# Delta-rule attention with experts: the triangular inverse of a 32-token chunk split into two 16x16 substitutions and a product on TensorE

## The chip, the cores and the metric

One of the cores of one Trainium2 chip runs the whole program. The metric is the device time of one execution in microseconds; lower is better.

## What is computed

One transformer block on 4096 tokens of width 256. Its attention part is a gated delta rule with 8 heads, 8 memories ("modes") per head, keys and values of 64, in a strict recurrence over the tokens:

```python
def step(S, inp):
    q_t, k_t, v_t, b_g, b_beta = inp
    S = S * jnp.exp(b_g)[..., None, None]
    kv = jnp.einsum('mbhk,mbhkv->mbhv', k_t, S)
    dv = (v_t[None] - kv) * b_beta[..., None]
    S = S + k_t[..., :, None] * dv[..., None, :]
    o_t = jnp.einsum('mbhk,mbhkv->mbhv', q_t, S)
    return (S, o_t)
```

Keys and queries are rotated by angles that are scaled per head and mode, and normalised. Outputs of the modes are mixed, gated and projected. Then follows a layer of 8 experts with top-2 routing and a capacity of 1024 rows each. Everything is float32.

## The kernel before

The program has three blocks. The first (attention and routing) walks 32 tiles of 128 tokens; each tile is done in two **halves** `(n, hh)` of four heads, that is 8 "quads" q (a head and four of its modes; the four modes stand in four groups of 32 partitions). The program counts halves as u = 2n + hh, and v = u - 1 is the half before. A tile has four **chunks** c of 32 tokens. The second block does the experts, the third combines their rows.

Within a chunk the recurrence is solved by matrices. For each of 128 problems (4 chunks, 8 quads, 4 modes) of a half, a unit lower triangular 32x32 matrix has to be inverted, and its columns scaled by beta. `solve` (L1259) does this on VectorE with one problem per partition: L1261 transposes the 32x32 blocks of the systems from `at` into `bd`, L1263 puts beta on the diagonal in PSUM (`last_two`), and then 31 steps j each multiply a column of the system by row j of the inverse (L1270) and subtract the product from the rows below (L1272). L1275 transposes the inverse to `tt`. Two small jobs are done between steps: `clip_decays` (j = 8) and `sum_decays` (j = 16) for the next tile in halves with hh = 1, and `take_logits` (j = 12) of the tile before in halves with hh = 0; the last waits for TensorE's routing product.

In software pipelining, the half v of which `solve` has just ended goes through its four chunks while the half u is prepared. For each chunk, one chain alternates between TensorE (PE), VectorE (DVE), ScalarE (ACT) and GpSimd (POOL):

- `memory_read` (PE L572, 32 matmuls): keys times state;
- `right_sides` (DVE L1288, L1291);
- `expand_te` (ACT L797): `tt` of the chunk spread into block-diagonal `te`;
- `corrections` (PE L589 and L595, two groups g of heads): `te` times the right sides, and queries times state;
- `decayed_corrections` (DVE L1298), `take_dv` (ACT L812), `fade` (POOL L1573: decay of the state);
- `update_and_outputs` (PE L608, L616), and `update_memories` (DVE L1307, L1309), after which the state is ready for the next chunk.

Between these, each engine's program has the preparation of u woven in by hand, in the order of its function `half`: angles (`turns_mod_1`, `add_low_turns`, `turns_end`), `decays`, key rotation, `beta_decays` (L1230), `turn_keys`, `queries_for_memories` (L1248, L1249), `chunk_systems` (L1256, L1257, out of the PE products `gram`, L533). PE also copies rows over the partitions (`rows`, L508, in three pairs per half), replicates units (L517), makes `columns` (L498) of the decays that ACT has spread in `roots` (L838), and does the projections of the next tile (L482, L544, L555, L490) and the routing (L633, L638).

Each engine has a queue in order; a wait holds up all that is behind it. The products that are not the memories' own go through two rotating pairs of PSUM banks: one pair is taken by ACT (`to_act`/`take`), one by DVE (`to_dve`/`full`/`free`), each bank in turn, so that PE must wait with a product until its bank's use before last has been read. The loop body over the tiles holds `half(n, 1)` and `half(n + 1, 0)`; each engine goes back to its start after the latter.

## Time and profile before

| | before |
|---|---|
| median of 3 runs | 7000.74 us (6998.04 to 7004.32) |
| the profiled execution | 6999.14 us, its span 6997.4 us |
| busy: PE / PE weight loads | 4452.0 / 3830.1 us (64% / 55% of the span) |
| busy: DVE | 5135.8 us (73%) |
| busy: ACT / POOL | 3430.8 / 2767.8 us (49% / 40%) |
| mean granted TensorE clock | 0.817 of full speed |

Busy times are sums over one execution. Timeline rows have a start and a length in us; one row may hold several instructions. PE writes two records for each float32 matmul of the program (and two for its weights): x64 is 32 matmuls. What stands in square brackets is how long the engine was idle before the row and what released it. A granted clock of 1.00 is 2.4 GHz, of 0.50 is 1.2 GHz.

### The profile page before, as it was taken

The page shows a single profiled execution, that of the slowest core. Times are in us where ns is not written, and L with a number is a line of the kernel's source. Part 1 is how long each engine was busy: PE and PEld are TensorE (multiplying, and loading weights), DVE is VectorE, ACT ScalarE, POOL GpSimd, SP SyncE. Part 2 cuts the span into 40 slices and gives each one's busy share as a digit, 9 for nine tenths or more (in the row PEclk, how much of TensorE's full clock was granted, in tenths as well). Part 3 has the DMA queues.
Part 4 walks back from the last instruction along what each step waited for, and adds up shares of the span by engine and source line. Part 5 has one row for each costly group of instructions (what it writes and reads, how often), then busy time and mean ns, then how long its engine had stood idle before and what let it go on. Part 6 is the DMA issues. An engine that isn't in the chain of part 4 may idle for free. (4 is left out here: it accounts for less than half of the span.)

```text
span 6997.4 us, 195918 instructions
## 1 busy us (share of the span) xinstructions
PE 4452.0 (64%) x78513; PEld 3830.1 (55%) x78513; DVE 5135.8 (73%) x9800; ACT 3430.8 (49%) x6010; POOL 2767.8 (40%) x1789
## 2 busy tenths in 40 slices
PE   1666666666666666666666666666666666655993
PEld 1555555555555555555565555555555655553662
DVE  4888778888887887878888888778888888881003
ACT  1555555555555555555555555555555555542220
POOL 3444343444343443434443434434344443434003
PEclk6878878888887788888888787887878887887997
DMA  2000000000000000000000000000000000002223
GB/s 88 2 5 5 6 5 5 5 5 3 4 5 5 5 5 6 5 5 5 5 3 5 5 5 5 5 6 5 5 5 5 3 5 5 5 27 95 72 72 105
DMA packets 77479, 109.71 MB, mean 16 GB/s; under 512 B 20576, under 2 KB 66208, under 8 KB 75424
## 3 DMA queue, kind: packets, MB, share of 16 engines
q1 hardware_dynamic: 67616, 71.42, 3.2%
q0 software_dynamic: 8960, 25.39, 1.2%
q8 instruction: 672, 11.01, 0.7%
q14 instruction: 231, 1.89, 0.1%
HBM read 57.89 MB, written 38.89 MB: 14 GB/s over the span
## 5 line engine op out<-in xcount | busy, mean ns | idle before, releaser
L1573 POOL TENSOR_TENSOR state<-state,gc_end 128x512 f32<-128x512 f32 x512 | 591.5, 1172 | 1852.4 <-PE bank L595 1811.9
L589 PE MATMUL bank<-rhs,te 128*64 128x64 f32 x8192 | 412.6, 254 | 765.9 <-DVE rhs L1291 490.0
L572 PE MATMUL bank<-state,ke 128*64 128x64 f32 x16384 | 656.1, 248 | 341.0 <-DVE outT L1309 221.4
L572 PEld LDWEIGHTS bank<-state,ke 128*64 128x64 f32 x16384 | 616.8, 160 | 415.8 <-DVE state L1307 237.1
L797 ACT ACTIVATE te<-tt 32x256 f32<-32x256 f32 x1024 | 421.9, 412 | 802.6 <-DVE tt L1275 792.0
L589 PEld LDWEIGHTS bank<-rhs,te 128*64 128x64 f32 x8192 | 345.0, 163 | 844.4 <-DVE rhs L1291 795.8
L608 PE MATMUL last_two<-dvs,kte 128*64 128x64 f32 x16384 | 658.9, 241 | 180.1 <-DVE dvs L1298 180.1
L1272 DVE TENSOR_TENSOR last_two<-last_two,prod 128x31 f32<-128x31 f32 (+15 forms) x1984 | 692.4, 349 | 68.2
L847 ACT ACTIVATE ke<-kq 32x512 f32<-32x512 f32 x1024 | 642.9, 628 | 201.7 <-DVE kq L1223 188.0
L1270 DVE TENSOR_TENSOR prod<-bd,last_two 128x31 f32<-128x31 f32 (+15 forms) x1984 | 671.1, 338 | 68.3
L608 PEld LDWEIGHTS last_two<-dvs,kte 128*64 128x64 f32 x16384 | 597.2, 154 | 196.5 <-DVE dvs L1298 187.3
L533 PE MATMUL bank<-kq,ke 128*64 128x64 f32 x16384 | 536.2, 227 | 199.8 <-DVE pw L1257 111.2
L804 ACT ACTIVATE kte<-kt 32x512 f32<-32x512 f32 x1024 | 641.9, 627 | 36.5 <-PE last_two L608 17.1
L533 PEld LDWEIGHTS bank<-kq,ke 128*64 128x64 f32 x16384 | 512.6, 142 | 214.0 <-issue 125.8
L1598 POOL TENSOR_TENSOR pw<-pw,w_quad 128x1024 f32<-128x1024 f32 x64 | 122.5, 1914 | 992.3 <-DVEq L1441 992.3
L812 ACT ACTIVATE dv<-bank 128x256 f32<-128x256 f32 x512 | 188.1, 379 | 571.0 <-DVE dvs L1298 561.2
L1307 DVE TENSOR_TENSOR state<-last_two,state 128x512 f32<-128x512 f32 x512 | 354.0, 691 | 116.5 <-POOL state L1573 77.0
L508 PE MATMUL bank<-row_group,select 128*128 128x128 f32 x3072 | 417.9, 290 | 29.7 <-DVE col L1186 23.9
L508 PEld LDWEIGHTS bank<-row_group,select 128*128 128x128 f32 x3072 | 375.7, 198 | 47.7 <-DVE col L1186 24.2
L1768 DVE TENSOR_TENSOR yrow<-last_two,b_row 128x256 f32<-128x256 f32 x64 | 27.2, 424 | 503.9 <-PE last_two L1722 503.9
L1586 POOL TENSOR_TENSOR tmp<-raw,cos_t 128x1024 f32<-128x1024 f32 x64 | 151.5, 2368 | 589.7 <-ACTq L888 589.7
L595 PE MATMUL bank<-qg,state 128*64 128x32 f32 x8192 | 374.4, 240 | 0.0
(257 smaller groups left out, 10221.1 us busy)
## 6 DMA issues: line engine op xcount, KB each, us to landing
w_sb<-in_L_ffn_W_dram SPq DMA_DIRECT2D x16, 1024.0 KB, 9.5
expert_rows<-ke SPq DMA_DIRECT2D x1, 8192.0 KB, 21.9
xrows<-expert_rows SPq DMA_DIRECT2D x16, 512.0 KB, 8.4
expert_outputs<-yrow POOLq DMA_DIRECT2D x16, 512.0 KB, 3.4
xt<-_attn_hidden_states_dram SPq DMA_DIRECT2D x32, 128.0 KB, 2.9
xr<-_attn_hidden_states_dram SPq DMA_DIRECT2D x32, 128.0 KB, 2.1
x_after_attention<-xr SPq DMA_DIRECT2D x32, 128.0 KB, 1.7
xo<-x_after_attention SPq DMA_DIRECT2D x32, 128.0 KB, 3.9
```

The source lines that it names most:

```text
L508: mm = pe.matmul(b[:, ql * P:ql * P + P], select[:, b4 * 4 + ql, :], row_group[:, group, :], start=True, stop=True)
L533: mm = pe.matmul(b[s, q * 2 * C:(q + 1) * 2 * C], ke[:, c, r, q, s], kq[:, r, q, :, c * C:c * C + C], start=(r == 0), stop=(r == 1))
L572: mm = pe.matmul(bank_mem[g][s, q % 4 * DK:q % 4 * DK + DK], ke[:, c, r, q, s], state[:, hh * HQ + q, r, :], start=(r == 0), stop=(r == 1))
L589: pe.matmul(bank_mem[g][s, q % 4 * DK:q % 4 * DK + DK], te[:, q, s], rhs[:, q, :], start=True, stop=True)
L595: mm = pe.matmul(out_bank(g, side), state[:, hh * HQ + q, r, :], qg[:, r, q, c * C:c * C + C], start=(j == 0 and r == 0), stop=False)
L608: mm = pe.matmul(bank_upd[g][s, (q % 4) * P + r * DK:(q % 4) * P + r * DK + DK], kte[:, r, q, s], dvs[:, q, :], start=True, stop=True)
L797: ins = act.activation(te[s, :, 32 * m:32 * m + 32], tt[s, c, :, :], ACT.Copy)
L804: ins = act.activation(kte[s, :, :, 32 * m:32 * m + 32].rearrange("p r q f -> p (r q) f"), kt[s, :, :, c * C:c * C + C].rearrange("p r q f ...
L847: ins = act.activation(ke[s, c, :, :, 32 * m:32 * m + 32].rearrange("p r q j -> p (r q) j"), kq[s, :, :, 0, c * C:c * C + C].rearrange("p ...
L1270: ln(dve.tensor_tensor(pr, a_prob[:, j + 1:C, j:j + 1].broadcast_to([P, rows, cols]), t_prob[:, j:j + 1, 0:cols].broadcast_to([P, rows, co ...
L1272: ln(dve.tensor_tensor(below, below, pr, ALU.subtract))
L1573: pool.tensor_tensor(sv, sv, gc_end[:, vh, 4 * g:4 * g + 4, c].unsqueeze(2).broadcast_to([P, 4, 2 * DK]), ALU.mult).then_inc(sem(f"state_f ...
```

## The change

The 32x32 triangular matrix is taken as two 16x16 diagonal blocks and a lower left block. `solve` inverts both diagonal blocks side by side in 15 steps on DVE (b = 2 blocks of HC = 16), and writes them transposed (`tt_blocks`) and not (`t_blocks`). The lower left block of the inverse is the product -B inv * L * A inv. It is made for each chunk by two groups of matmuls, `cut_products` (32 matmuls, through a bank of ACT, taken by `take_cut`) and `lower_left` (32 matmuls, through a bank of DVE, taken by `finish_inverse`, which is what `tt_ready` now tells). These are put one chunk ahead of their use: chunk 0 at the end of the half of its `solve`, chunk 1 around the update of chunk 0, chunks 2 and 3 around the update of chunk 1. `queries_for_memories` goes behind `solve`, together with its PE `rows`; `sum_decays` goes behind the substitution; ACT's spread of the decays, PE's `columns` and POOL's `group_rows` go later. `take_logits` stays within `solve`, at step 8 of 15, `clip_decays` at 9. `beta_decays` is split, so that the lower 16 columns can take the mask with them. In the last block four loads of `xo` become one.

```diff
@@ tiles
-        prod = sb("prod", [P, HH * P])
+        cut = sb("cut", [P, 2, HQ, C])
...
+        at = raw[:].rearrange("p s h t -> p (s h t)").rearrange("p (c q i) -> p c q i", c=NC, q=HQ)
...
+        a_blocks = bd_flat.rearrange("p (i x j) -> p i x j", x=4, j=HC)[:, :, 0:4:3, :]
+        prod = dvs[:].rearrange("p q v -> p (q v)")
...
@@ tensor
+            def cut_products(u, c):
+                pe.wait_ge(sem("t_turned"), u + 1)
+                def emit(b):
+                    pe.sem_inc(sem("pe_held"), 1)
+                    for q in range(HQ):
+                        for s in MODES:
+                            top = slice(s.start, s.start + HC)
+                            mm = pe.matmul(b[s, q * HC:(q + 1) * HC], at[top, c, q, :], t_blocks[top, c, q, :], start=True, stop=True)
+                    return mm
+                to_act(emit)
+            def lower_left(u, c):
+                pe.wait_ge(sem("cut_ready"), 4 * u + c + 1)
+                def emit(b):
+                    pe.sem_inc(sem("pe_held"), 1)
+                    for q in range(HQ):
+                        for s in MODES:
+                            mm = pe.matmul(b[s, q * HC:(q + 1) * HC], cut[s, c % 2, q, :], tt_blocks[s, c, q, :], start=True, stop=True)
+                    return mm
+                to_dve(emit)
...
+                if not first:
+                    corrections(v, vh, 0)
                 if hh == 0:
                     columns(n)
-                if hh == 1:
-                    pe.wait_ge(sem("logits_taken"), since("logits_taken", n))
-                if not first:
-                    memory_read(v, vh, 0)
-                    corrections(v, vh, 0)
+                if not first:
+                    cut_products(v, 1)
                     update_and_outputs(v, 0)
+                    lower_left(v, 1)
                     memory_read(v, vh, 1)
                 pe.wait_ge(sem("groups_ready"), n + 1)
                 rows(hh)
                 if not first:
                     corrections(v, vh, 1)
+                    cut_products(v, 2)
+                    cut_products(v, 3)
                     update_and_outputs(v, 1)
+                    lower_left(v, 2)
+                    lower_left(v, 3)
                 replicate(u, (0, 1), to_dve)
...
-                rows(4 + hh)
...
+                rows(4 + hh)
+                cut_products(u, 0)
+                if hh == 0 and not first:
+                    pe.wait_ge(sem("logits_taken"), since("logits_taken", n))
+                memory_read(u, hh, 0)
+                lower_left(u, 0)
@@ scalar
+            def take_cut(v, c):
+                act.wait_ge(sem("t_turned"), v + 1)
+                act.activation(tt[:, c, :, 0:HC], tt_blocks[:, c], ACT.Copy, scale=upper)
+                take(lambda b: act.activation(cut[:, c % 2, :, 0:HC], b[:, 0:HQ * HC].rearrange("p (q j) -> p q j", q=HQ), ACT.Copy, scale=minus_lower))
+                act.sem_inc(sem("cut_ready"), 1)
             def expand_te(v, c):
+                act.wait_ge(sem("tt_ready"), 4 * v + c + 1)
...
@@ vector
-                for j in range(C - 1):
+                for j in range(HC - 1):
                     for do in meanwhile.get(j, ()):
                         do()
-                    rows, cols = C - 1 - j, j + 1
...
+                    rows, cols = HC - 1 - j, j + 1
+                    pr = prod[:, 0:rows * 2 * cols].rearrange("p (i b c) -> p i b c", b=2, c=cols)
+                    below = t_prob[:, j + 1:HC, :, 0:cols]
+                    ln(dve.tensor_tensor(pr, a_blocks[:, j + 1:HC, :, j:j + 1].broadcast_to([P, rows, 2, cols]),
+                                         t_prob[:, j:j + 1, :, 0:cols].broadcast_to([P, rows, 2, cols]), ALU.mult))
                     ln(dve.tensor_tensor(below, below, pr, ALU.subtract))
...
+                ln(dve.transpose(tt_blocks.rearrange("p c q i -> p i (c q)"), t_rows))
+                vec(dve.transpose(t_blocks.rearrange("p c q j -> p j (c q)"), t_prob.rearrange("p i b j -> p j b i")), "t_turned", u + 1)
+            def finish_inverse(v, c):
+                b = full()
+                free(dve.scalar_tensor_tensor(tt[:, c, :, HC:C], tt_blocks[:, c], lower,
+                                              b[:, 0:HQ * HC].rearrange("p (q i) -> p q i", q=HQ), ALU.mult, ALU.add))
+                dve.sem_inc(sem("tt_ready"), 1)
...
                 memories(right_sides, 0)
                 turns_mod_1(u)
+                memories(finish, 0)
+                add_low_turns(u)
                 memories(decayed_corrections, 0)
-                add_low_turns(u)
                 if hh == 0:
                     take_columns()
+                memories(finish, 1)
...
                 decays(u, hh, 1)
+                memories(finish, 2)
+                memories(finish, 3)
                 memories(right_sides, 2)
...
-                queries_for_memories(u, first)
...
+                solve(u, hh, first, meanwhile)
+                if hh == 1 and not last:
+                    sum_decays(n2)
+                queries_for_memories(u, first)
```

PE's order from a half's first correction to its second memory read. In the program before:

```order
L572 MATMUL bank<-state,ke 64x64 x32
L585 REGISTER_ALU
L589 MATMUL bank<-rhs,te 64x64 x8
L595 MATMUL bank<-qg,state 64x32 x8
L589 MATMUL bank<-rhs,te 64x64 x8
L595 MATMUL bank<-qg,state 64x32 x8
L608 MATMUL last_two<-dvs,kte 64x64 x16
L612 REGISTER_ALU
L616 MATMUL bank<-pw,dv 64x32 x4
L608 MATMUL last_two<-dvs,kte 64x64 x16
L616 MATMUL bank<-pw,dv 64x32 x4
L572 MATMUL bank<-state,ke 64x64 x32
```

In the changed program, from `columns` on (L671 is `cut_products`, L683 `lower_left`, L617 and L625 the update, L581 the memory read):

```order
L507 MATMUL bank<-cmat,xg 128x32 x4
L461 REGISTER_ALU
L671 MATMUL bank<-bd,raw 32x16 x32
L617 MATMUL last_two<-dvs,kte 64x64 x16
L621 REGISTER_ALU
L625 MATMUL bank<-pw,dv 64x32 x4
L617 MATMUL last_two<-dvs,kte 64x64 x16
L625 MATMUL bank<-pw,dv 64x32 x4
L683 MATMUL bank<-bd,cut 32x16 x32
L581 MATMUL bank<-state,ke 64x64 x32
```

A group of 32 small matmuls now stands before the update of chunk 0 and another behind it; `columns` has moved from ahead of the first memory read to here.

PE's order a little later, from the second correction of chunk 1 to the memory read of chunk 2. In the program before:

```order
L595 MATMUL bank<-qg,state 64x32 x8
L608 MATMUL last_two<-dvs,kte 64x64 x16
L616 MATMUL bank<-pw,dv 64x32 x4
L608 MATMUL last_two<-dvs,kte 64x64 x16
L616 MATMUL bank<-pw,dv 64x32 x4
L459 REGISTER_ALU
L517 MATMUL bank<-unit,spread 128x512 x2
L572 MATMUL bank<-state,ke 64x64 x32
```

In the changed program:

```order
L604 MATMUL bank<-qg,state 64x32 x8
L671 MATMUL bank<-bd,raw 32x16 x32
L461 REGISTER_ALU
L671 MATMUL bank<-bd,raw 32x16 x32
L617 MATMUL last_two<-dvs,kte 64x64 x16
L625 MATMUL bank<-pw,dv 64x32 x4
L617 MATMUL last_two<-dvs,kte 64x64 x16
L625 MATMUL bank<-pw,dv 64x32 x4
L468 REGISTER_ALU
L683 MATMUL bank<-bd,cut 32x16 x32
L677 REGISTER_ALU
L683 MATMUL bank<-bd,cut 32x16 x32
```

Four groups of 32 have come in between the correction of chunk 1 and `replicate` (L526 now), behind which the memory read of chunk 2 stands as before.

DVE's order from the decayed corrections of chunk 0 to the update of its memories, in the program before:

```order
L1298 TENSOR_TENSOR dvs<-bank,dec_end 128x256 x2
L1173 TENSOR_TENSOR tmp<-tmp,kq 128x1024
L1115 REGISTER_ALU
L1174 TENSOR_SCALAR tmp<-tmp 128x1024
L1115 REGISTER_ALU
L1118 REGISTER_ALU
L1186 COPY col<-bank 128x128
L1307 TENSOR_TENSOR state<-last_two,state 128x512
```

In the changed program, from the low turns on (L1353 is `finish_inverse`, L1387 the first row of `update_memories`):

```order
L1241 TENSOR_TENSOR tmp<-tmp,sin_t 128x1024
L1182 REGISTER_ALU
L1242 TENSOR_SCALAR tmp<-tmp 128x1024
L1182 REGISTER_ALU
L1377 REGISTER_ALU
L1378 TENSOR_TENSOR dvs<-bank,dec_end 128x256 x2
L1185 REGISTER_ALU
L1254 COPY col<-bank 128x128
L1191 REGISTER_ALU
L1185 REGISTER_ALU
L1353 SCALAR_TENSOR_TENSOR tt<-bd,cmat,bank 128x8x16
L1387 TENSOR_TENSOR state<-last_two,state 128x512
```

The low turns have gone ahead of the decayed corrections, and `finish_inverse` of chunk 1 has come in ahead of the update of chunk 0. `finish_inverse` of chunk 0 stands just ahead of the low turns.

## Rows read from the trace of the kernel before

**Rows 1.** The profile's page: busy us, share of the span and instructions by engine.
```profile
PE 4452.0 (64%) x78513; PEld 3830.1 (55%) x78513; DVE 5135.8 (73%) x9800; ACT 3430.8 (49%) x6010; POOL 2767.8 (40%) x1789
```
**Rows 2.** The page's costliest groups: the substitution's two operations.
```profile
L1272 DVE TENSOR_TENSOR last_two<-last_two,prod 128x31 f32<-128x31 f32 (+15 forms) x1984 | 692.4, 349 | 68.2
L1270 DVE TENSOR_TENSOR prod<-bd,last_two 128x31 f32<-128x31 f32 (+15 forms) x1984 | 671.1, 338 | 68.3
```
**Rows 3.** Timeline of DVE, queries and the substitution of an hh = 1 half.
```profile
2012.09 0.69 DVE L1248 TENSOR_TENSOR qg<-kq,bank 128x512 f32<-128x512 f32 x1 [0.20 <-PE bank L508]
...
2025.77 1.99 DVE L1261 STREAM_TRANSPOSE bd<-cos_t 128x1024 f32<-128x1024 f32 x1 [0.15 <-DVE pw L1257]
...
2028.15 0.20 DVE L1270 TENSOR_TENSOR prod<-bd,last_two 128x31 f32<-128x31 f32 x1
...
2040.43 0.42 DVE L1270 TENSOR_TENSOR prod<-bd,last_two 128x256 f32<-128x256 f32 x1
2040.88 0.43 DVE L1272 TENSOR_TENSOR last_two<-last_two,prod 128x256 f32<-128x256 f32 x1
2041.35 1.55 DVE L1144 TENSOR_TENSOR_SCAN gb<-cmat,gb 64x128 f32<-64x128 f32 x1
...
2056.22 0.43 DVE L1288 TENSOR_TENSOR bank<-bank,eg_col 128x256 f32<-128x256 f32 x1
...
2060.14 0.42 DVE L1298 TENSOR_TENSOR dvs<-bank,dec_end 128x256 f32<-128x256 f32 x1
```
**Rows 4.** Timeline of DVE, the substitution of the hh = 0 half that follows.
```profile
2119.41 1.98 DVE L1261 STREAM_TRANSPOSE bd<-cos_t 128x1024 f32<-128x1024 f32 x1
...
2136.37 0.17 DVE L1325 TENSOR_TENSOR lg<-bank,br_row 128x8 f32 x1 [6.08 <-PE bank L638]
...
2156.69 0.43 DVE L1288 TENSOR_TENSOR bank<-bank,eg_col 128x256 f32<-128x256 f32 x1 [3.33 <-issue]
```
**Rows 5.** Timeline behind both substitutions: updates and third right sides on DVE, `te` on ACT.
```profile
2065.05 0.69 DVE L1307 TENSOR_TENSOR state<-last_two,state 128x512 f32<-128x512 f32 x1
...
2079.13 0.43 DVE L1288 TENSOR_TENSOR bank<-bank,eg_col 128x256 f32<-128x256 f32 x1 [1.05 <-PE bank L572]
...
2164.53 0.69 DVE L1307 TENSOR_TENSOR state<-last_two,state 128x512 f32<-128x512 f32 x1 [0.22 <-DVE tmp L1174]
...
2056.10 1.69 ACT L797 ACTIVATE te<-tt 32x256 f32<-32x256 f32 x4 [8.97 <-DVE tt L1275]
```
**Rows 6.** Timeline of PE: small matmuls in a row, columns, memory read, first corrections.
```profile
2005.81 0.61 PE L595 MATMUL bank<-qg,state 128*64 128x32 f32 x16
2006.25 0.66 PE L589 MATMUL bank<-rhs,te 128*64 128x64 f32 x16
...
2044.46 1.91 PE L498 MATMUL bank<-cmat,xg 128*128 128x32 f32 x8 [6.96 <-ACT xg L838]
2046.30 3.68 PE L572 MATMUL bank<-state,ke 128*64 128x64 f32 x64
2057.94 1.12 PE L589 MATMUL bank<-rhs,te 128*64 128x64 f32 x16 [7.95 <-ACT te L797]
...
2061.34 1.21 PE L608 MATMUL last_two<-dvs,kte 128*64 128x64 f32 x32
```
**Rows 7.** Timeline of PE, chunk 1: update, replicate, memory read of chunk 2.
```profile
2072.06 1.13 PE L608 MATMUL last_two<-dvs,kte 128*64 128x64 f32 x32
...
2074.64 1.13 PE L517 MATMUL bank<-unit,spread 128*128 128x512 f32 x2
2076.88 1.13 PE L517 MATMUL bank<-unit,spread 128*128 128x512 f32 x2 [1.11 <-DVE dec L1195]
2077.93 2.09 PE L572 MATMUL bank<-state,ke 128*64 128x64 f32 x64
```
**Rows 8.** Busy time and granted clock by stretch, the fourth last number the clock.
```profile
2057.90:2061.00 3.10, 3.06 (x58) 3.09 (x60) 2.47 (x4) 0.33 (x1) 0.95 (x1) 0.50 0.03 5
2066.00:2080.00 14.00, 12.77 (x293) 10.81 (x293) 10.91 (x21) 9.81 (x16) 2.06 (x2) 1.00 0.01 4
```

More of the change, by code:

```diff
@@ L28 @@
 C = 32
+HC = C // 2
 NT = T // P
@@ L957, in _ @@
                 take_dv(v, c)
+                for c2 in ((1,), (2, 3), (), ())[c]:
+                    take_cut(v, c2)
                 if c < NC - 1:
```

136 lines of the change are left out of this document (79 added, 57 removed).

## The prediction

> **What bounds the kernel now.** I read the page's busy times first [rows 1]: DVE is busy 73% of the span, PE 64%, ACT 49%, POOL 40%. No engine is full, so the chain has to be followed. The page's groups name the largest thing on DVE [rows 2]: the two operations of the substitution, 671.1 + 692.4 = 1363.5 us. The timeline then says what each stretch waits for. In the substitution DVE works without a break, and the other engines are waiting for it: ACT was idle 8.97 us before it could spread `tt` [rows 5], PE 7.95 us before the corrections [rows 6]. Behind the substitution the chunk chain takes over; there DVE has its own fill work, and PE is almost full (12.77 of 14.00 us busy in one such stretch [rows 8]). So DVE sets the pace while it substitutes, and PE and DVE by turns in the chunks. Both kinds of half are needed, since they differ: with hh = 0, `take_logits` holds DVE 6.08 us within the substitution [rows 4], and the loop's turn costs another 3.33 us behind it (cause "issue").
>
> I work everything out for one pair of halves (a tile) and multiply by 31.5, as there are 63 halves with a memory half behind a substitution. The profiled execution took 6999 us, 1.6 us under the median, so no correction is due.
>
> **Part 1: what the substitution gives back.** An operation of 31 elements takes 0.20 us, one of 256 takes 0.42 or 0.43, and starts follow each other by 0.45 and 0.47 [rows 3]. That is 0.19 us (multiply) or 0.20 us (subtract) and 1.04 ns an element, start to start. The new 15 steps handle 2 x 680 = 1360 elements in each operation: 15 x 0.39 + 2 x 1360 x 1.04 ns = 8.7 us, against 23.4 for 31 steps with 5456. Two transposes of 512 elements replace one of 1024; from the 1.99 us of L1261 for 1024 elements [rows 3] I take 1.05 each.
>
> - hh = 1. Before: from the first transpose to the right sides 2056.22 - 2025.77 = 30.45 us [rows 3], and 3.15 us of queries ahead of it (four of 0.69 and their gaps [rows 3]): 33.6. After: transposes 2.4, steps 8.7, clip 1.0, transposes 2.2, scan 1.55 [rows 3], queries 3.1: 18.9. Gain 14.7.
> - hh = 0. Before: 2156.69 - 2119.41 = 37.3 [rows 4], and 3.15: 40.4. After: the routing product for `take_logits` comes out of a chain (POOL's `pw`, turns and squares, PE, ACT, PE) that starts where the substitution starts and doesn't get shorter; it lands 2136.37 - 2119.41 = 17.0 us in [rows 4]. DVE reaches step 8 after 7 us and waits 10. Then 0.2 + 4.0 (seven steps) + 2.2 + queries 3.1 + loop 3.3: 29.8. Gain 10.6.
>
> Together **-25.3 us a pair**.
>
> **Part 2: what one group of 32 small matmuls costs.** The trace has no 32x16 matmul. The nearest row is L595, which streams 32 columns: 8 matmuls took 2006.25 - 2005.81 = 0.44 us [rows 6], 55 ns each, so 32 make 1.76. Upper bound: L572, also 32 matmuls, took 2.09 us at the full clock and 3.68 at the half [rows 6, 7]. Lower bound: an estimate of half of L595's, 0.88 us, if the weights (32 columns instead of 64) are what fills those 55 ns. I take **1.75 us**, as L595 is nearest in what it streams. Rule against row: the Trainium skill (TensorE: Matmul & The Clock Gate, back-to-back issue gap) says that starts never come closer than about 25 ns however few columns; by two records a matmul that is an estimate of 1.6 us, and the sum below would be 7112 instead of 7155. The 27 ns a record of L595 agree with it.
>
> **Part 3: the first chain, from the right sides to the update of chunk 0.** Before it took 2065.05 - 2056.22 = 8.8 us (hh = 0 half) and 2164.53 - 2156.69 = 7.8 us [rows 3, 4, 5]. `tt` was whole at its start, and the low turns covered PE's update. Now the chain is: right sides and mod-1 turns 3.8 (together they fill 2056.22 to 2060.14 [rows 3]) and `finish_inverse` 0.35, since all of these stand ahead on DVE; `te` 1.7 and its signal 0.15; corrections 2061.34 - 57.94 = 3.4, at the half clock that the rows show after such a gap (0.50 [rows 8]; PE would have been idle about 5 us here); `cut_products` of chunk 1, 2.0 (between full and half clock); update, two groups, 2.5 (2072.06 to 2074.64 is 2.6 with small waits [rows 7]); `lower_left` 1.75; landing and `finish_inverse` 0.55. Sum 16.2, and with `columns` (1.9, L498 [rows 6]) 18.1. DVE has nothing to fill the wait: the low turns have gone ahead, and the update of chunk 0, though ready, is queued behind `finish_inverse` of chunk 1. Cost 9.3 + 8.4 = **+17.7 us a pair**. `finish_inverse` of chunk 0 waits for nothing: its two groups and ACT's cut lie beside the queries and right sides.
>
> **Part 4: the second chain, to the right sides of chunk 2.** Before: 2079.13 - 2065.05 = 14.1 us [rows 5]. From 2072.06 on PE ran update, replicate and memory read with one gap of 1.11 [rows 7]. Four groups come in, 7.0 us; they swallow that gap. Net 5.9, and 0.1 for the wait for a bank before the last: **+12.0 us a pair**.
>
> **Part 5: the small rest.** `beta_decays` in four pieces instead of two, 0.3 a half: **+0.6**. ACT's `take_cut`, two operations of 128 elements a chunk, lies beside PE's groups; with it gone as cover nothing else would be late, so 0. One clearing less on ACT, 0: ACT waited there. POOL's `group_rows` moves between two fades; rows of PE ask for it 3 us after the update, 0. The merged `xo` loads: SP only, and the last block waits for gathers, 0. The queue in which a wait is added is DVE's (four of `finish_inverse`), and its price is parts 3 and 4.
>
> **Sum:** -25.3 + 17.7 + 12.0 + 0.6 = +5.0 us a pair, times 31.5 = +156. **Forecast 7155 us**, 2.2% slower: DVE's saved work comes back as waits for PE. Its own range is 7020 to 7350 (group cost 1.6 to 2.05; clock after the gap).
>
> **The rivals.**
>
> *The small matmuls are cheap (faster).* Place: the six groups on the chain in each half. If a group costs 0.88 us, the first chain shrinks by 2 and the second by 2 (there DVE's decays set the end instead), 8.1 a pair: 5.0 - 8.1 = -3.1, 6900 us; with the clock staying up, 6780. It decides from 1.2 us a group, 37 ns a matmul. For it: only 32 weight columns, and L595's 55 ns double with the clock (L572: 2.09 and 3.68), as array work does and a fixed issue cost would not. Against: L589 streams twice L595's columns, and its 16 records took 0.66 us against 0.61 [rows 6], so the stream is not the bound there; whether it is the weights or a floor for each record, no row tells.
>
> *DVE stays the bound (faster by far).* If the chains of parts 3 and 4 were hidden but for the new DVE work (about 2 us a half), -25.3 + 4.6 a pair gives 6350 us. For it: the busy share. Against: DVE's order in parts 3 and 4 has nothing to cover with.
>
> *The clock stays up.* Corrections at 1.9 instead of 3.4, columns at 1.0: -3.9 a pair, leaving +1.1: 7035 us. For it: PE has shorter gaps. Against: after 7.95 us idle the clock was 0.50 [rows 8], and 5 us is nearer to that than to the 1.11 us gap at 1.00.
>
> *Row tiles hinder each other (slower by far).* The four modes of a group work in different row groups and write one bank. If each record had to end before the next starts, at about 0.2 us a record (L595's 16 records took 0.61 us, their starts spread over 0.41 of it [rows 6]), a group takes 13 us; six on the chain add 67 us a half, and the kernel ends near 11,000 us. The Trainium skill (TensorEngine Tiling (Array Packing), restrictions, PSUM pressure) says that different row tiles cannot access the same bank at once. No row here has two row tiles; every matmul before uses all 128 rows.
>
> **Numbers.** Forecast 0.52; cheap matmuls 0.22; DVE bound 0.07; clock up 0.14 (a part of it within the bounds of no change); row tiles 0.05. About 0.2% (14 us) is what a measurement of this kernel can tell from none. So faster 0.32, same 0.05, slower 0.63. The range leaves out the far cases and the tails of the near ones: 6850 to 7350.
>
> **What would show it.** Right: DVE busy falls to about 4370 us (-1363 + 490 + 110), PE's matmul records rise by 32,768 to 111,000; a DVE wait of 5 to 7 us before `finish_inverse` of chunk 1 in each half, released by PE's L683; a wait of about 3 us at the update of chunk 1 and 2.5 at the right sides of chunk 2; `take_logits` waits 10 us. Wrong: groups of 32 under 1.2 us; a clock of 1.00 in the first corrections; DVE idle less than 20 us a half.

## The result and the profile after

| | before | changed |
|---|---|---|
| median | 7002.5 us (4 runs) | 7382.9 us (4 runs, 7376.6 to 7392.9) |
| ratio | | 1.0544, 95% interval 1.0526 to 1.0563 |
| span of the profiled execution | 6997.4 us | 7374.9 us |
| mean granted clock | 0.817 | 0.794 |

The kernel got 5.4% slower; 2.2% was forecast, and the time lies above the range. The page's row that answers to [rows 1]:

```profile
PE 5202.4 (71%) x111281; PEld 4513.9 (61%) x111281; DVE 4365.2 (59%) x8200; ACT 3583.1 (49%) x6458; POOL 2749.4 (37%) x1790
```

VectorE gave back 771 us of work, and the kernel lost 377. The timeline of DVE in an hh = 1 half, from its substitution to the right sides of chunk 2 (answers to [rows 3, 5]):

```profile
2145.73 1.05 DVE L1347 STREAM_TRANSPOSE bd<-last_two 128x512 f32<-128x512 f32 x1
...
2153.48 0.43 DVE L1368 TENSOR_TENSOR bank<-bank,eg_col 128x256 f32<-128x256 f32 x1 [0.37 <-DVE qg L1319]
...
2171.50 0.35 DVE L1353 SCALAR_TENSOR_TENSOR tt<-bd,cmat,bank 128x128 f32<-128x128 f32 x1 [6.11 <-PE bank L683]
2172.08 0.69 DVE L1387 TENSOR_TENSOR state<-last_two,state 128x512 f32<-128x512 f32 x1 [0.23 <-DVE tt L1353]
...
2185.54 0.69 DVE L1387 TENSOR_TENSOR state<-last_two,state 128x512 f32<-128x512 f32 x1 [2.04 <-PE last_two L617]
...
2196.55 0.43 DVE L1368 TENSOR_TENSOR bank<-bank,eg_col 128x256 f32<-128x256 f32 x1 [4.67 <-PE bank L581]
```

I cut each half at four events of DVE: first subtraction of the substitution, first store of the right sides, update of chunk 0, first store of the right sides of chunk 2. The stretches in us, hh = 1 half / hh = 0 half (a half is named after its substitution); the upper two rows are one pair near 2000 us, the lower two the means of 61 halves (all but the first and the last two):

| | substitution to right sides | first chain | second chain | rest |
|---|---|---|---|---|
| before, one pair | 28.3 / 35.1 | 8.4 / 7.4 | 14.6 / 14.6 | 42.4 / 43.5 |
| changed, one pair | 17.5 / 28.6 | 18.1 / 16.1 | 24.9 / 23.6 | 39.9 / 38.4 |
| before, mean | 28.6 / 35.5 | 8.4 / 7.4 | 14.5 / 14.6 | 42.5 / 41.3 |
| changed, mean | 17.1 / 28.5 | 18.0 / 15.3 | 24.1 / 23.1 | 40.2 / 38.5 |

The single pair makes the chains look longer than they are on average, so the account goes by the means, and so do all lengths of chains below. The queries (3.15 us a half) moved from the rest to the first column. With them counted in both kernels, a pair gains 24.9 in the substitution, and loses 1.1 in the rest, 17.6 in the first chain and 18.2 in the second: 12.0, or 378 us in 31.5 pairs.

The second chain on PE in an hh = 1 half:

```profile
2173.14 3.68 PE L581 MATMUL bank<-state,ke 128*64 128x64 f32 x64 [1.71 <-DVE outT L1389]
2176.75 2.94 PE L517 MATMUL bank<-row_group,select 128*128 128x128 f32 x16
...
2181.61 1.21 PE L671 MATMUL bank<-bd,raw 16*32 16x16 f32 x104
2183.98 0.38 PE L671 MATMUL bank<-bd,raw 16*32 16x16 f32 x24 [1.16 <-issue]
2184.28 1.15 PE L617 MATMUL last_two<-dvs,kte 128*64 128x64 f32 x32
...
2185.47 1.96 PE L617 MATMUL last_two<-dvs,kte 128*64 128x64 f32 x32
2187.22 0.59 PE L625 MATMUL bank<-pw,dv 128*64 128x32 f32 x8
2187.74 1.05 PE L683 MATMUL bank<-bd,cut 32*32 32x16 f32 x64
2189.68 1.05 PE L683 MATMUL bank<-bd,cut 32*32 32x16 f32 x64 [0.88 <-issue]
2191.36 3.78 PE L526 MATMUL bank<-unit,spread 128*128 128x512 f32 x4 [0.63 <-DVE tt L1353]
2195.07 2.36 PE L581 MATMUL bank<-state,ke 128*64 128x64 f32 x64
```

The same stretch before:

```profile
2165.59 2.10 PE L572 MATMUL bank<-state,ke 128*64 128x64 f32 x64 [0.67 <-DVE outT L1309]
2167.62 2.05 PE L508 MATMUL bank<-row_group,select 128*128 128x128 f32 x16
...
2171.54 1.13 PE L608 MATMUL last_two<-dvs,kte 128*64 128x64 f32 x32
```

and the granted clock by stretch, changed kernel (fourth last number):

```profile
2159.60:2165.00 5.40, 5.40 (x74) 5.27 (x75) 1.10 (x3) 2.78 (x9) 2.48 (x4) 0.50 0.02 3
2165.00:2173.10 8.10, 6.43 (x209) 6.22 (x208) 1.60 (x5) 1.50 (x4) 1.27 (x5) 0.50 0.02 4
2173.10:2176.80 3.70, 3.66 (x65) 3.57 (x65) 3.23 (x6) 3.60 (x7) 0.00 (x0) 0.50 0.00 0
2176.80:2181.60 4.80, 4.80 (x81) 4.65 (x80) 1.62 (x4) 4.13 (x5) 0.66 (x1) 0.81 0.02 3
...
2187.70:2195.10 7.40, 5.88 (x137) 3.12 (x134) 3.50 (x7) 3.61 (x8) 0.00 (x0) 0.50 0.02 4
```

Before, it had been 0.50 in the first corrections and was 1.00 from the memory read of chunk 1 on:

```profile
2157.60:2161.20 3.60, 3.57 (x66) 3.52 (x66) 3.20 (x5) 0.00 (x0) 1.45 (x1) 0.50 0.00 0
2161.20:2165.60 4.40, 3.73 (x83) 3.64 (x82) 3.86 (x6) 3.25 (x8) 1.30 (x2) 0.69 0.02 4
2165.60:2169.70 4.10, 4.10 (x82) 3.86 (x82) 3.60 (x7) 3.56 (x5) 0.00 (x0) 1.00 0.01 4
```

So two things stand in the second chain. New work: the four groups take 1.21 + 0.38 + 1.05 + 1.05 = 3.7 us in this half. And old work runs at the lower clock: memory read 3.68 against 2.10, rows 2.94 against 2.05. The means over all halves, in us a pair, divide the 18.2:

| second chain on PE, mean, a pair | before | changed |
|---|---|---|
| old matmuls (memory reads, rows, corrections, update, replicate) | 24.0 | 31.6 |
| the groups | | 6.3 |
| idle, "issue" | | 2.8 |
| waits for a DVE bank that `decays` reads | 2.2 | 2.1 |
| waits for `finish_inverse` | | 1.4 |
| wait for the outputs ahead of the memory read | 1.9 | 2.1 |
| granted clock, hh = 1 / hh = 0 | 1.00 / 1.00 | 0.73 / 0.80 |

The wait of `replicate` for its bank has become one of `lower_left`, mostly in hh = 0 halves. The old matmuls' 7.6 us are the largest item: memory reads and replicate grow by 2.8 each, rows and update by some 1.0 each, and the corrections not at all. "Issue" is not new in itself: over the whole execution PE is idle for it 100.5 us in the changed kernel (64.3 of them at the two new lines) and 119.0 us in the one before, all at its memory reads (L572). Which of these a different order could avoid is what the experiments ask.

### The profile page after: what moved, and what is told of

Read it like the earlier page. It is cut to its first block and busy times, and to the rows that moved or that the text cites. A ratio compares the mean times of both kernels' runs of the same rounds, so it can differ in the third digit from the quotient of the medians.

```text
span 7374.9 us, 260540 instructions
## 1 busy us (share of the span) xinstructions
PE 5202.4 (71%) x111281; PEld 4513.9 (61%) x111281; DVE 4365.2 (59%) x8200; ACT 3583.1 (49%) x6458; POOL 2749.4 (37%) x1790
## 3 DMA queue, kind: packets, MB, share of 16 engines
q8 instruction: 928, 15.20, 0.9%
## 5 line engine op out<-in xcount | busy, mean ns | idle before, releaser
L581 PEld LDWEIGHTS bank<-state,ke 128*64 128x64 f32 x16384 | 657.6, 171 | 368.6 <-DVE state L1387 271.7
L581 PE MATMUL bank<-state,ke 128*64 128x64 f32 x16384 | 694.4, 258 | 256.9 <-DVE outT L1389 256.4
L617 PE MATMUL last_two<-dvs,kte 128*64 128x64 f32 x16384 | 720.2, 253 | 212.7 <-DVE dvs L1378 176.8
L598 PE MATMUL bank<-rhs,te 128*64 128x64 f32 x8192 | 437.5, 265 | 542.9 <-ACT te L856 428.2
L617 PEld LDWEIGHTS last_two<-dvs,kte 128*64 128x64 f32 x16384 | 652.9, 165 | 226.6 <-DVE dvs L1378 184.0
L598 PEld LDWEIGHTS bank<-rhs,te 128*64 128x64 f32 x8192 | 367.6, 173 | 615.4 <-ACT te L856 427.8
L863 ACT ACTIVATE kte<-kt 32x512 f32<-32x512 f32 x1024 | 642.0, 627 | 19.4 <-ACT h2T L1000 5.5
L517 PE MATMUL bank<-row_group,select 128*128 128x128 f32 x3072 | 535.2, 345 | 26.5 <-DVE col L1254 23.2
L517 PEld LDWEIGHTS bank<-row_group,select 128*128 128x128 f32 x3072 | 504.3, 255 | 60.0 <-DVE col L1254 23.4
L1387 DVE TENSOR_TENSOR state<-last_two,state 128x512 f32<-128x512 f32 x512 | 354.0, 691 | 299.3 <-PE last_two L617 196.6
L1368 DVE TENSOR_TENSOR bank<-bank,eg_col 128x256 f32<-128x256 f32 x512 | 221.3, 432 | 440.1 <-PE bank L581 298.3
L1378 DVE TENSOR_TENSOR dvs<-bank,dec_end 128x256 f32<-128x256 f32 x512 | 217.3, 424 | 356.5 <-PE bank L604 347.7
L604 PE MATMUL bank<-qg,state 128*64 128x32 f32 x8192 | 403.1, 250 | 0.0
L526 PE MATMUL bank<-unit,spread 128*128 128x512 f32 x512 | 356.0, 834 | 45.6 <-DVE tt L1353 44.6
## 6 DMA issues: line engine op xcount, KB each, us to landing
expert_rows<-ke SPq DMA_DIRECT2D x1, 8192.0 KB, 21.9
```

The source lines that it names most:

```text
L517: mm = pe.matmul(b[:, ql * P:ql * P + P], select[:, b4 * 4 + ql, :], row_group[:, group, :], start=True, stop=True)
L526: to(lambda b: pe.matmul(b[:, :], spread[:, s, :], unit[:].rearrange("p h t -> p (h t)"), start=True, stop=True))
L581: mm = pe.matmul(bank_mem[g][s, q % 4 * DK:q % 4 * DK + DK], ke[:, c, r, q, s], state[:, hh * HQ + q, r, :], start=(r == 0), stop=(r == 1))
L598: pe.matmul(bank_mem[g][s, q % 4 * DK:q % 4 * DK + DK], te[:, q, s], rhs[:, q, :], start=True, stop=True)
L604: mm = pe.matmul(out_bank(g, side), state[:, hh * HQ + q, r, :], qg[:, r, q, c * C:c * C + C], start=(j == 0 and r == 0), stop=False)
L617: mm = pe.matmul(bank_upd[g][s, (q % 4) * P + r * DK:(q % 4) * P + r * DK + DK], kte[:, r, q, s], dvs[:, q, :], start=True, stop=True)
```

## The experiments

Each time below was taken beside runs of the kernel before on the same chip, 7023 to 7027 us; ratios are to those. The changed kernel was not run again there. At its ratio of 1.0544 it stands at 7405 to 7409 us on that scale, and gains against it are counted from there, although the expectations count from 7382.

### One small matmul in eight, and each twice

```diff
-for q in range(HQ):            # both groups
+for q in (0,):                 # e1_few
+for q in 2 * tuple(range(HQ)): # e1_twice
```

> Leaves out 7 of 8 of the new small matmuls (quad 0 alone is done in cut_products and lower_left); all groups, banks, waits and orders stay. Three theories of the 12 us a pair by which the changed kernel is slower. (a) The groups' own time on PE: a group is 0.7 us at the full clock and about 1.0 at the half; six on the chain of each half, so about 4.5 us a half goes, 7382 to about 7100. (b) The places: the update of chunk 0 queued behind finish_inverse of chunk 1, te behind finish_inverse, banks; then the matmuls' number hardly matters, and the time stays above 7250. (c) Code loading: PE's issue gaps of about 1 us (three a pair) come from the added instructions; then they vanish, another 3 us a pair, about 100 us, beyond (a). If the clock is held down by small matmuls standing in for large ones, the granted clock would rise here.

> Every group of small matmuls is emitted twice into the same bank (the same result). (a) A slope of the groups' own time: plus 6 x 0.8 us a half, 7382 to about 7680, and more than twice the issue gaps if (c) code loading counts. (b) places: the added work partly fills waits, under 7550.

Measured: 7175 us (ratio 1.0215, 1.019 to 1.024; clock 0.792) and 8045 us (1.1453, 1.143 to 1.1475; clock 0.768). The first kernel makes one quad's product in eight, so its output is not the reference's. It lies between its two theories: with almost no small matmuls it is 231 us faster than the changed kernel, and still 2% slower than the one before. That rest lies in the places, the added waits and the clock, which did not rise: in the second chain it is 0.76 / 0.83, and the old matmuls take 30.4 us a pair there (31.6 in the changed kernel, 24.0 before). Nor did "issue" vanish, as the third theory wanted: it is 101.7 us against 100.5, so the number of small matmuls is not what makes those gaps in the changed kernel.

The second groups cost 639 us, far over the 300 expected; the 231 us for seven eighths make 264 for the whole first set, so they cost 2.4 times as much. PE's time "issue" at the two lines is 235.0 + 209.1 us there, against 33.9 + 30.4 in the changed kernel. Matmuls do not add linearly.

### `finish_inverse` of chunk 1 behind the update of chunk 0

```diff
-memories(finish, 1)
 ...
 memories(update_memories, 0)
+memories(finish, 1)
```

> DVE does finish_inverse of chunk 1 behind the update of chunk 0's memories instead of ahead of it; nothing else moves. If the place is what costs (b), the update starts when PE's update lands, some 2.7 us sooner in each half: minus 170 us, about 7210. If the first chain is not where the excess over the forecast is, the rest of the 12 us a pair stays. Rival: te of chunk 1 comes later on ACT and gives it back, 7380.

Measured: 7258 us (1.0338, 1.0314 to 1.0363), 148 us less; 170 were expected. DVE now updates chunk 0 while PE makes the product. The first chain fell from 18.0 / 15.3 to 14.0 / 12.3, but the second grew from 24.1 / 23.1 to 25.3 / 24.6: of 7.0 us a pair 2.6 came back, as the rival had it in part. The queued update is nearly two fifths of the loss; the prediction had named this place, with no price of its own.

### TensorE kept busy before the first corrections

```diff
+warm(16)   # shortened: 16 matmuls 128x128x128 of constants, into a bank of ACT
 corrections(v, vh, 0)
```

> The changed kernel with 16 more matmuls (128x128x128, from constants, result unused) just ahead of the corrections of chunk 0, where PE waits about 7 us for the right sides. Theory of the clock: the granted clock is at its lower level in the first corrections and the first update because PE sat idle before; kept busy it is at 1.00, the first corrections, the update (4.3 us against 2.5) and the groups shorten by 3 to 4 us per half, and the time falls by 150 to 250 us to 7130 to 7230. Rival, that the second chain is long through instructions that come in late and through waits for bank and finish: under 60 us, 7320 or more; more work for PE could also cost it something.

Measured: 7314 us (1.0408, 1.0345 to 1.047), 95 us less, under the 150 expected. The mean clock rose to 0.835, and in the first chain from 0.56 / 0.67 to 0.85 / 0.82. But in an hh = 1 half, which has `columns` there, it fell again: 0.71 from the first group to the end of the second, 0.56 in the next memory read. The first chain went from 18.0 / 15.3 to 15.2 / 16.1; in hh = 0 halves PE comes to the added matmuls only 3.7 us into that chain and is busy with them for 6.0 us. The second took 22.7 / 23.9 where it had 24.1 / 23.1, no gain to speak of. A busy stretch ahead did not carry the clock over what follows.

### All products ahead of the chains

```diff
                 cut_products(u, 0)
                 memory_read(u, hh, 0)
                 lower_left(u, 0)
+                cut_products(u, 1)
+                cut_products(u, 2)
+                lower_left(u, 1)
+                cut_products(u, 3)
                 ...
+                    lower_left(v, 2)
+                    lower_left(v, 3)
                     corrections(v, vh, 0)
```

(the groups in the chains are gone; on DVE the low turns go back behind the decayed corrections and all four `finish_inverse` stand behind the right sides and the mod-1 turns)

> All four chunks' products are made before the first corrections, in the time in which PE waits for te (cut_products 0, memory read 0, lower_left 0, cut_products 1 and 2, lower_left 1, cut_products 3, then in the next half lower_left 2 and 3); DVE does finish_inverse 0 and 1 right behind the right sides, 2 and 3 behind the mod-1 turns, and the low turns go back behind the decayed corrections. If the places in the chain are the cause (b), the first chain returns to 10 or 11 us from 18.6 and 16.6, the second to 14 or 15 from 24.5 and 23.1: minus 16 us a half, near 6400, faster than both kernels. If the clock is the cause, PE is still at the half clock in corrections, update and memory read, and only the groups' own time goes: about 7000.

Measured: 7009 us (0.9974, 0.9964 to 0.9984), 600 us above what the theory of the places gave. It is the rival's 7000, but by luck: the rival had PE at the half clock in the second chain's work, and that chain is back at 15.9 / 14.5, with a clock of 0.92 / 1.00. The first takes 17.5 / 20.7. PE in an hh = 0 half:

```profile
2141.96 0.72 PE L683 MATMUL bank<-bd,cut 32*32 32x16 f32 x64
2142.55 0.63 PE L671 MATMUL bank<-bd,raw 16*32 16x16 f32 x54
2145.06 1.30 PE L671 MATMUL bank<-bd,raw 16*32 16x16 f32 x74 [1.88 <-issue]
2146.22 0.93 PE L683 MATMUL bank<-bd,cut 32*32 32x16 f32 x52
2148.79 0.34 PE L683 MATMUL bank<-bd,cut 32*32 32x16 f32 x10 [1.64 <-issue]
...
2149.01 1.04 PE L671 MATMUL bank<-bd,raw 16*32 16x16 f32 x62
2154.87 1.47 PE L683 MATMUL bank<-bd,cut 32*32 32x16 f32 x89 [4.83 <-issue]
2157.76 0.73 PE L683 MATMUL bank<-bd,cut 32*32 32x16 f32 x39 [1.41 <-issue]
2158.41 1.12 PE L598 MATMUL bank<-rhs,te 128*64 128x64 f32 x16
```

A group runs at 10 ns a record and then PE stands still without waiting for anything shown. The DMA view for 2140 to 2165:

```profile
q8 instruction: 7, 0.11, 2.2%
```

Seven packets of instructions of 16 KB in 25 us. How many matmuls a packet holds can be read from the next run, whose page shows 704 packets (11.53 MB) where this one shows 928 (15.20 MB), for 14,336 fewer matmuls: 256 bytes each, 64 to a packet, 128 records. That is 28 ns a record supplied, against 10 used. The new theory: the small matmuls outrun PE's supply of instructions.

The packets' own times bear it out. The four gaps above that lie in this window after 2143 end at 2145.06, 2148.79, 2154.87 and 2157.76, and the packets just before them ended at 2143.48, 2147.24, 2152.76 and 2156.30: 1.5 to 2.1 us earlier each time. Over the whole execution the 183 gaps of more than 1 us at the two lines end a median of 1.42 us after a packet of q8 has ended (90% of them 1.25 to 2.11); for instants taken at random that distance has a median of 3.5 us and 90% of them spread from 0.3 to 20. In the run with each group twice it is 205 gaps and 1.40 us. The 31 gaps of the run with one in eight end 2.5 to 3.1 us after a packet, so those are of another kind.

### The same with one small matmul in eight

> The version with all four chunks' lower left products ahead of the chains, now with one quarter head in eight: 32 of the 256 small matmuls of a group pair are left (the lower left blocks of the other heads are stale, so the output is not the reference's). Theory A, that PE's instructions come in slower than these small matmuls run, and that the idle time 'issue' of PE (about 390 us at the second product's line, up to 4.8 us at a stretch, in the version with all of them) is what the early place costs: that idle time falls below 60 us, the first chain comes back to about 9 us, and the time falls by 400 to 550 us against the 7009 us of the early version, to 6450 to 6600. Rival B, that the early version is held by ScalarE's copies, by the wait for take_logits or by the clock, and the issue gaps only lie beside these: under 200 us of gain, 6800 or more.

Measured: 6518 us (0.9275, 0.9253 to 0.9298). 491 us less, within what the theory gave and far over its rival. The waits at the second product (total us, number, longest), first of the version with all of them:

```profile
PE bank L683 <- issue: 395.0, 161, 5.0
```

The row of the version with few in the view by groups:

```profile
L683 PE MATMUL bank<-bd,cut 32*32 32x16 f32 x2048 | 72.2, 204 | 275.3 <-DVE tt L1347 151.2 <-DVE qg L1313 51.3 <-issue 37.2
```

395 us of "issue" became 37, and the first chain 11.1 / 11.1, above the 9 expected. The groups' own time went too: their rows at the two lines take 131 us busy where they took 492. So this run does not divide the 491 us between gaps and matmuls; the next one bears on that. It also prices the idea: with the products almost free, it would be worth 7%.

### As many small matmuls, four times as wide

```diff
-b[s, q*HC:(q+1)*HC],     ..., t_blocks[top, c, q, :]
+b[s, q*4*HC:(q+1)*4*HC], ..., t_blocks[top, c, q, :].unsqueeze(1).broadcast_to([HC, 4, HC])
```

> The early version (7009 us) with as many small matmuls as before, each with its moving operand repeated four times, so 64 columns instead of 16; only the first 16 are read. Theory A, that PE's instructions come in at a pace of their own, about 29 ns for a record of these lines (gaps end every 126 to 129 records and 3.7 us apart in the trace), and that the small matmuls, at 10 ns a record, outrun them: the wider ones take the room of the gaps. Idle time 'issue' at the second product's line falls from 395 us to under 100 while its busy time rises by about as much, and the time is 6960 to 7080. Rival B, that a gap comes with each such matmul whatever its length, or that the time is TensorE's own: the extra columns come on top, at least 1 us for each of eight groups in each of 63 halves, 7500 or more.

Measured: 6969 us (0.9913, 0.9893 to 0.9934): 40 us *less* with four times the columns.

```profile
L683 PE MATMUL bank<-bd,cut 32*32 32x64 f32 x16384 | 411.0, 262 | 299.7 <-issue 290.9 <-DVE qg L1313 7.6 <-ACTq L847 0.2
```

The columns went into time that was lost anyway, so TensorE's own work is not what bounds this run of groups. But "issue" fell from 395 to 291 and not under 100; the supply is not one fixed rate that a wider matmul fills. And the mean clock rose from 0.816 to 0.853: corrections and updates of all chunks (L598, L604, L617) took 1390 us busy instead of 1521.

### `take_logits` behind the substitution

```diff
-meanwhile[8] = [lambda: take_logits(n - 1)]
 solve(u, hh, first, meanwhile)
+take_logits(n - 1)
```

> The changed kernel with take_logits moved out of the substitution to just behind it. It waits 10.9 us there once per pair of halves, for router products that PE ends at 2044.7 us of the trace, while PE's first group of products could start at 2048.3 behind rows, and starts at 2051.4. If this wait only sets that start: 3 us per pair, 100 us, 7280. Rival, that the substitution's end was late for all that follows, 8 us or more per pair: 7130 or less. Rival, that PE is behind anyway: 0.

> The early version (all four chunks' products ahead of the chains, 7009 us) with take_logits behind the substitution: the same 3 to 4.5 us per pair, 6870 to 6920, which would beat both kernels. If the early version is held by PE's incoming instructions alone, the earlier start is worth as much; if it is held behind by the router's own chain: under 40 us.

Measured: 7281 us (1.0361, 1.0336 to 1.0386) and 6867 us (0.9776, 0.9757 to 0.9795), 128 and 142 us less, or 4.1 and 4.5 a pair, where 3 and 3 to 4.5 were expected. The hh = 0 half reaches its right sides 23.9 us after the start of its substitution instead of 28.5. `take_logits` waited 10.8 us there; 4.6 came off the path. That the rest stays because PE is held by the router's products and `rows`, after which the first group stands, fits the order but was not tested.

### Products of chunks 2 and 3 in the second chain

From the 6867 us version: chunks 0 and 1 stay ahead, first products of 2 and 3 go behind the corrections of chunk 0.

```diff
+cut_products(v, 2)
+cut_products(v, 3)
 update_and_outputs(v, 0)
 memory_read(v, vh, 1)
 rows(hh)
 corrections(v, vh, 1)
+lower_left(v, 2)
 update_and_outputs(v, 1)
+lower_left(v, 3)
 replicate(u, (0, 1), to_dve)
```

> The early version with take_logits behind the substitution (6867 us), with the products of chunks 0 and 1 left ahead of the chains and those of chunks 2 and 3 put into the second chain where PE waits anyway: first products behind the corrections of chunk 0, second ones behind the corrections and the update of chunk 1. Theory A (instructions come in at their own pace, so short matmuls in one long run cost 29 ns each and between longer ones 10): the first chain falls from 20.6 and 16.8 us to 12 to 13, the second grows from 15 to 17 to 19; 6650 to 6750. Rival, that a group costs in the second chain what it cost in the changed kernel (9 to 10 us there for three): the second chain is 21 or more, 6850 or more.

> As the split version, with the first products of chunks 0 and 1 ahead of the eight matmuls of rows(4 + hh). In the half with the router, rows end 3.6 us after the substitution could; in the other half rows lie in TensorE's idle time before the substitution ends, and now come behind it. If the router's half gains 3 us and the other loses as much: within 0.2% of the split version. If the queries, which need the rows, can wait: 30 to 90 us less than it.

Measured: 7109 us (1.0096, 1.0065 to 1.0127) and 7119 us (1.0119, 1.0102 to 1.0137). The first missed its theory by some 360 us and met its rival. The second is within 0.2% of it, one of its two cases. The first chain did fall, from 17.2 / 20.5 to 13.0 / 13.8, but the second went from 15.7 / 14.5 to 24.4 / 23.8. On PE:

```profile
2107.64 0.72 PE L683 MATMUL bank<-bd,cut 32*32 32x16 f32 x64 [1.96 <-DVE dec L1263]
...
2112.85 0.72 PE L683 MATMUL bank<-bd,cut 32*32 32x16 f32 x64 [2.04 <-issue]
2114.53 3.47 PE L526 MATMUL bank<-unit,spread 128*128 128x512 f32 x4 [0.96 <-DVE tt L1353]
```

A group that comes behind `rows` in the rotation of DVE's two banks can start only when `decays` has read them, and the memory read of chunk 2 is queued behind it. Over the execution it waits 136.5 us for that. Moving `rows` of the queries behind the products gained nothing.

### The second products ahead of `rows`

```diff
 memory_read(v, vh, 1)
+lower_left(v, 2)
+lower_left(v, 3)
 rows(hh)
 corrections(v, vh, 1)
-lower_left(v, 2)
 update_and_outputs(v, 1)
-lower_left(v, 3)
```

(on DVE both `finish_inverse` behind the right sides of chunk 1; on ACT both cuts ahead of `expand_kte`)

> The split version (7109 us) with one thing moved: the second products of chunks 2 and 3 stand behind the memory read of chunk 1 and ahead of rows, and VectorE's finish_inverse of both behind the right sides of chunk 1, ahead of the decays; ScalarE takes the cuts before expand_kte. In the split version the second products stood between rows and replicate, and waited there 2.0 and 2.4 us for a bank that the decays hold (PE L683 <- DVE dec 136.5 us in all), 1.0 us for finish_inverse at replicate, and 1.7 to 2.0 us of issue; the memory read of chunk 2 is queued behind them. Theory C, that the place in VectorE's bank rotation made the second chain 23 us long there, and in the changed kernel too: the second chain falls from 23 to 24 us to 16 to 18, the first stays at 13, and the time is 6560 to 6700, below the early version's 6867. Rival A alone, that incoming instructions set it wherever the groups stand: the gaps move to memory read, rows and corrections of chunk 1, the second chain stays above 20 us, 6950 or more.

Measured: **6738 us** (0.9588, 0.9572 to 0.9604), 371 us less by order alone, and 4.1% under the kernel before; a little above what was expected. The second chain takes 19.3 / 19.4 (16 to 18 expected), 9.4 us a pair less. The second products and the first corrections behind the groups, in the split version:

```profile
L683 PE MATMUL bank<-bd,cut 32*32 32x16 f32 x16384 | 203.5, 185 | 282.3 <-DVE dec L1263 136.5 <-issue 127.7 <-DVE qg L1319 16.0
L598 PE MATMUL bank<-rhs,te 128*64 128x64 f32 x8192 | 421.0, 258 | 357.0 <-issue 133.8 <-DVE rhs L1371 116.7 <-ACT te L856 106.5
```

and here:

```profile
L683 PE MATMUL bank<-bd,cut 32*32 32x16 f32 x16384 | 193.0, 180 | 45.5 <-issue 25.5 <-DVE qg L1319 15.5
L598 PE MATMUL bank<-rhs,te 128*64 128x64 f32 x8192 | 419.8, 257 | 368.9 <-issue 137.5 <-DVE rhs L1371 120.1 <-ACT te L856 111.3
```

The wait for `decays` at L683 is gone, and so are 102 us of its "issue"; the first corrections keep theirs. PE runs the same instructions in 4914 us of busy time instead of 5242, with the mean clock at 0.845 instead of 0.793. So the place in the rotation of the banks is one part of the gain, and the clock that came with the new order another; the three queues were changed together, and no run parts them.

### Wide matmuls in the changed kernel and in the best one

> The changed kernel (7383 us) with each small matmul's moving operand repeated four times (64 columns instead of 16, the first 16 read); number and places stay. If 16-column matmuls count little for the clock and so hold it at 0.50 through the first and second chain: the mean clock rises from 0.79 to 0.83 or more, memory read, rows and update of chunk 1 in the second chain are back near 2.1, 2.05 and 2.6 us, and although a group takes about 0.5 us longer (six on the chain in each half, 190 us) the time stays within 7250 to 7400. Rival, that only the idle times set the clock: it stays at 0.80 or less, and the extra columns come on top, 7550 or more.

> The version with the second products ahead of rows (6738 us), with 32 columns in each small matmul instead of 16. If narrow matmuls hold the clock down: the clock rises a little above 0.845, and the time falls by 20 to 60 us, 6680 to 6720. Rival, that the columns only cost: 6750 to 6800.

> The same with 64 columns. In the early version this took 40 us off (7009 to 6969, clock 0.816 to 0.853), where gaps hid the extra columns. Here eight groups a half stand with fewer gaps: if the clock is what it bought, 6660 to 6720; if the gaps were what made it free, 6800 or more.

Measured: 7297 us (1.039, 1.0372 to 1.0407; clock 0.840), 6750 us (0.9614; 0.856) and 6733 us (0.9595; 0.873). In the changed kernel, in the same places, four times the columns take 108 us off. In an hh = 0 half:

```profile
2043.21 1.10 PE L671 MATMUL bank<-bd,raw 16*32 16x64 f32 x64
2044.23 1.15 PE L617 MATMUL last_two<-dvs,kte 128*64 128x64 f32 x32
...
2049.59 3.31 PE L581 MATMUL bank<-state,ke 128*64 128x64 f32 x64 [1.81 <-DVE outT L1389]
2052.84 2.35 PE L517 MATMUL bank<-row_group,select 128*128 128x128 f32 x16
...
2066.32 1.96 PE L526 MATMUL bank<-unit,spread 128*128 128x512 f32 x4 [0.28 <-DVE tt L1353]
2068.20 2.09 PE L581 MATMUL bank<-state,ke 128*64 128x64 f32 x64
```

This half shows the first update at the full clock (1.15 a row; 1.98 in halves at 0.50), but that is not the rule: it takes 2.5 us in 13 of the 30 hh = 0 halves here and in 14 of them with narrow groups, and in hh = 1 halves 4.1 to 4.5 us here and 4.4 to 4.5 there. The gain is in the second chain, 20.4 / 21.9 instead of 24.1 / 23.1, while the first grew from 18.0 / 15.3 to 19.0 / 16.1. In the second chain the clock is 0.96 / 0.90, and the old matmuls take 26.3 us a pair: of the 7.6 us by which they had slowed down, 5.3 came back, against 2.4 more for the groups themselves. So the clock with narrow groups in these places is what slowed the old matmuls. What it is in these stretches that holds the clock down is not shown: PE is also less idle in this chain with wide groups (6.4 us a pair instead of 8.5), and with an eighth of the narrow ones the clock stayed almost as low (0.76 / 0.83).

In the best version the clock rose in the same way and the time hardly moved. With 32 columns it is the rival's 6750, and with 64 it lies between the two cases, and its interval overlaps that of the narrow ones: there the extra columns cost what the clock gives.

## Why the prediction was wrong

The direction was right (slower), and so was the account of where time is won and lost; the size was not, and nearly all of the miss comes from one term.

**Right.** DVE busy 4365 us (forecast 4370), 111,281 records of PE. Part 1: 24.9 us a pair given back, 25.3 forecast. Part 3: 17.6 us, 17.7 forecast, with the wait before `finish_inverse` of chunk 1 where the prediction put it (6.0 us in hh = 1 halves and 4.7 in the others; 5 to 7 forecast), and 0.50 in the first corrections. `take_logits` waits 10.8 us (10 forecast). Part 5 and all else: 1.1, 0.6 forecast.

**Part 2 was wrong, and its error hid.** A group of 32 takes a row of 0.72 us at the full clock, and the next row can start 0.65 us after it; at the half clock it is 1.05. For the full clock that is under the prediction's lower bound of 0.88. The sum took 1.75 from L595, with 27 ns a record where these have 10. The cheap matmuls' rival was thus right in its condition and wrong in its result (6900). Part 3 came out right only in its sum, by luck: the two groups there are 2.1 us in an hh = 1 half and 1.7 in the other, not 3.7, while the update ran wholly at the half clock in every hh = 1 half, 4.4 us of it where 2.5 was taken (3.5 on average in the others). The rule of the Trainium skill (TensorE: Matmul & The Clock Gate, back-to-back issue gap) that starts are never closer than about 25 ns is contradicted by these rows: 64 records in 0.65 us. (By that rule the prediction's sum would be 7108 and not 7112: five groups at 1.75 stand in it a half.) The rival of hindering row tiles fell: all four modes of a group write one bank, in 0.65 us.

**Part 4 failed:** 12.0 us a pair forecast, 18.2 measured; 6.2 x 31.5 = 195 us of the miss of 228. The step that failed is "Four groups come in, 7.0 us" on top of a chain that otherwise stays as long as in [rows 7], at the full clock. The groups with their gaps and waits come to 6.3 us a half, near 7.0 by accident: 3.2 of matmuls, 1.4 of "issue", 1.0 of waits for a bank (0.1 forecast) and 0.7 for `finish_inverse`. What was put at nothing is that the old matmuls of this chain slow down: 3.8 us a half, with the granted clock at 0.73 / 0.80 instead of 1.00. Its signs failed with it: the wait at the update of chunk 1 is 2.1 / 0.9 us (3 forecast), the one at the right sides of chunk 2 4.6 / 4.7 (2.5 forecast). Wide groups in the same places (e12) brought back 5.3 of the 7.6 us a pair with the clock. The prediction had the clock only in the first corrections and in a rival in which it stays up; that it could stay down longer was in no case.

**Open:** what keeps the clock down in the second chain. Wide groups raise it, a busy stretch ahead (e3) does not raise it there, and leaving out seven groups' matmuls in eight (e1_few) does not either; `columns`, which moved in between corrections and update in hh = 1 halves, was not tried alone. The long gaps at "issue" in long runs of groups go with the instruction packets (e1_twice, e4_early, e4_early_few) and not with TensorE's work (e10). Why wider matmuls fill only a part of them, and what the "issue" of the changed kernel and of e1_few is, no run shows.

## What to carry to other kernels

A long unbroken run of many small matmuls is paid in PE's instructions, not its array time: count the bytes of instructions there, and part the run by longer matmuls. When a product goes into a rotating pair of banks, look whose read it queues behind: order in the three queues, this place among it, moved this kernel from 7109 to 6738 us. And cost what a change adds to a chain together with the clock of all that stands behind it there. Last, measure a chain over all its repeats: the one pair read first here gave 7.4 us for the miss of Part 4, the mean 6.2.

## What was not expected of the hardware

- 32 matmuls of 16 or 32 rows and 16 columns, in four row groups and one bank, make a row of 0.72 us, and the next row starts 0.65 us after it: 20 ns a matmul, 10 a record.
- The granted clock stayed at 0.50 through 11.9 us in which PE was busy without a break (2159.58 to 2171.43: corrections, `columns`, a group, update, a group). In the changed kernel's hh = 1 halves it is at 1.00 again 10.6 to 19.1 us after the start of the first corrections, in its hh = 0 halves, which have no `columns` there, after 3.3 to 16.8; in the kernel before after 3.2 to 6.6.
- PE stands idle at "issue" for up to 4.8 us within a run of short matmuls, while packets of 64 matmuls' instructions come some 3.6 us apart, and such a gap ends some 1.4 us after a packet.
